# The bf16 conversion of the FFN's weights, issued in 64 pieces at every fourth step of attention instead of in 16 transfers

## The chip, the cores and the metric

The kernel runs on the 8 cores of one Trainium2 chip, one batch element on each core. A time is the device time of the slowest core in microseconds. The kernel before took 906.47 us (median of 3 runs).

## The reference

```python
# x: (8, 2048, 1024) f32; 16 heads of 64; FFN width 4096
def _L0_attn_ref(x, W_qkv, W_out):
    qkv = jnp.einsum('bsd,ndh->bnsh', x, W_qkv)
    q, k, v = jnp.split(qkv, 3, axis=-1)
    attn = jnp.einsum('bnqh,bnkh->bnqk', q, k) * scale
    attn = jax.nn.softmax(attn + causal_mask, axis=-1)
    out = jnp.einsum('bnqk,bnkh->bnqh', attn, v)
    out = out.reshape(B, -1, S)
    return jnp.einsum('bds,nhd->bsd', out, W_out)

def _L0_ffn_ref(x, w1, b1, w2, b2):
    h = jax.nn.relu(jnp.einsum('bsd,dw->bsw', x, w1) + b1)
    return jnp.einsum('bsw,wd->bsd', h, w2) + b2

x = x + _L0_attn_ref(_layernorm(x), L0_attn_W_qkv, L0_attn_W_out)
x = x + _L0_ffn_ref(_layernorm(x), L0_ffn_w1, L0_ffn_b1, L0_ffn_w2, L0_ffn_b2)
```

Attention's output is reshaped so that the last product sums W_out over heads and head positions; the kernel therefore needs no matmul for it, only a factor per element (WBp_sb).

## The kernel before

**Stages.** Each core works on a sequence of 2048 tokens by 1024 features. First come layer norm, transposes, the values of all heads and the queries and keys of the first pair of heads. Then comes attention, pair by pair: 8 pairs of heads, and in each 40 steps (`STEPS`), a step being a block of 512 queries (four of them) against a block of 128 keys as far as the causal mask lets it. Then comes the second layer norm and the FFN in 4 groups of 512 tokens, each with 32 blocks of the first product (line 514) and 8 of the second (line 536).

**A step of attention.** TensorE computes the scores of both heads two steps ahead (`score`, line 395, and the mask at line 407), ScalarE takes their exponential (line 626), and TensorE multiplies it with the values (`pv`, line 425). Between them TensorE computes the next pair's queries and keys (`qk`, line 371). The string `ORDER` writes out by hand how many halves of `pv` ("p") and pieces of `qk` ("f") stand in each step. VectorE evicts the next pair's queries (line 665) and applies the softmax's sums. TensorE counts finished scores in the semaphore `pe_s` (one per step, 320 in all), finished `qk` groups in `pe_f` (four per pair), and finished `pv` steps in `pe_pv`. Pair 7 has no next pair, so its steps hold no `qk`.

**The FFN's weights.** w1 and w2 lie in HBM as f32. The matmuls want bf16, and the conversion is done by transfers from HBM to HBM issued by GpSimd (POOL): w1 into `w1b` (line 281) and w2 into `w2b` (line 285), 8 transfers each of 1 MB of bf16. They are issued in `gpsimd`, in the loop that loads the queries' and keys' weights of pairs 1 to 7 into `wstage` (line 273). In its rounds 4, 5, 6 and 7, two transfers of w1 and two of w2 follow the load. Round 4 begins when the values are done, and rounds 5, 6 and 7 when the pairs 1, 2 and 3 have their queries and keys (`pe_f` 4, 8, 12). Everything that GpSimd issues goes through one queue (q0).

**Who waits for them.** The SyncE (SP) queue, in `sync`, waits at line 213 for all of w1, then at line 215 for `pe_f` 24 and 28, and loads the first two blocks of w1b (line 208). At line 217 it waits for all of w2 and loads w2b in four parts (line 222): two when `lnf_sb` is free, two when the last `pv` is done. GpSimd waits for both at its end (lines 295 and 296), behind the 16 additions of b2 to x (line 292), each of which waits for VectorE's second layer norm.

```python
STEPS = [(qb, j) for qb in range(4) for j in range(4 * qb + 4)]
NST = len(STEPS)
```

Of the kernel before, what the change touches and what calls it, by code (L numbers as in the profile page):

```python
# [11 lines left out]
AP = bass.AP  # L12

S = 2048
D = 1024
# [4 lines left out]
DC = 8  # L20
W1N = 4096
NWW = 32
# [7 lines left out]
NP = 5  # L30

WLAG, FLAG = 4, 7


ORDER = """
# [40 lines left out]
def build_program():  # L76
# [6 lines left out]
    w1_d = nc.dram_tensor("w1", [D, W1N], F32, kind="ExternalInput")  # L83
    b1_d = nc.dram_tensor("b1", [128, NWW], F32, kind="ExternalInput")
    w2_d = nc.dram_tensor("w2", [W1N, D], F32, kind="ExternalInput")
# [5 lines left out]
    w1b_d = nc.dram_tensor("w1b", [8, 128, DC * 512], BF16, kind="Internal")  # L91
    w2b_d = nc.dram_tensor("w2b", [128, NWW * D], BF16, kind="Internal")

    with ExitStack() as ctx:
# [3 lines left out]
        def sem(name):  # L98
            return ctx.enter_context(nc.semaphore(name))
# [60 lines left out]
        def slotap(s, dims):  # L160
            return AP(wstage, s * 1024, [[8 * 1024, 128]] + dims)
# [8 lines left out]
        w1_cast, w2_cast = sem("w1_cast"), sem("w2_cast")  # L170
# [6 lines left out]
        pe_s, pe_fh, pe_f = sem("pe_s"), sem("pe_fh"), sem("pe_f")  # L177
# [21 lines left out]
        def sync(e):  # L199
            for c in range(TC):  # L200
                e.dma_start(
                    x_sb[:, c, :], AP(x_d, c * 128 * D, [[D, 128], [1, D]])
                ).then_inc(x_in[c], 16)
            e.dma_start(b1c_sb[:, :], b1_d.ap()).then_inc(b1_in, 16)

            def w1_load(n):

                e.dma_start(
                    slotap(4 * (n % 2), [[1, DC * 512]]),
                    AP(w1b_d, (n % 8) * 128 * DC * 512, [[DC * 512, 128], [1, DC * 512]]),  # L210
                ).then_inc(w1b_in[n % 2], 16)

            e.wait_ge(w1_cast, 16 * 8)
            for n in range(2):
                e.wait_ge(pe_f, 24 + 4 * n)
                w1_load(n)
            e.wait_ge(w2_cast, 16 * 8)
            for i in range(4):
                if i == 2:
                    e.wait_ge(pe_pv, NSTEP)  # L220
                buf = lnf_sb if i < 2 else w2hi_sb
                e.dma_start(
                    AP(buf, (i % 2) * 8 * D, [[16 * D, 128], [1, 8 * D]]),
                    AP(w2b_d, i * 8 * D, [[NWW * D, 128], [1, 8 * D]]),
                ).then_inc(w2b_in[i], 16)
            for g in range(NG):
                for n in range(8 * g + 2, min(8 * g + 10, 8 * NG)):
                    e.wait_ge(pe_f1, 4 * (n - 2) + 4)
                    w1_load(n)
                for i in range(8 * g, 8 * g + 8):  # L230
                    e.wait_ge(dve_y, i + 1)
                    e.dma_start(
                        AP(y_d, (i // 2) * 128 * D + 512 * (i % 2), [[D, 128], [1, 512]]),
                        x_sb[:, i // 2, 512 * (i % 2):512 * (i % 2) + 512],
                    ).then_inc(y_out, 16)
            e.wait_ge(b1_in, 16)
            for c in range(TC):
                e.wait_ge(x_in[c], 16)
            for i in range(4):
                e.wait_ge(w2b_in[i], 16)  # L240
            for i in range(2):
                e.wait_ge(w1b_in[i], 16 * 16)
            e.wait_ge(y_out, 16 * 8 * NG)

        def gpsimd(e):
            e.dma_start(identb[:, :], identf_d.ap()).then_inc(cst_in, 16)
            e.dma_start(
                wqk0_sb[:, :], AP(wqk_d, 0, [[DC * 256, 128], [1, DC * 256]])
            ).then_inc(wqk0_in, 16)
            for h in range(2):  # L250
                if h == 1:
                    e.wait_ge(x_in[11], 16)
                    e.dma_start(maskd[:, :], maskd_d.ap()).then_inc(mask_in, 16)
                e.dma_start(
                    slotap(4 * h, [[1, DC * 512]]),
                    AP(wv_d, h * 128 * DC * 512, [[DC * 512, 128], [1, DC * 512]]),
                ).then_inc(wv_in[h], 16)
            e.wait_ge(x_in[TC - 1], 16)
            for k in range(4):
                e.dma_start(  # L260
                    wout_sb[:, 2 * k:2 * k + 2, :],
                    AP(wout_d, k * 256 * D, [[D, 128], [128 * D, 2], [1, D]]),
                ).then_inc(wout_in[k], 16)
            e.wait_ge(dve_ln, TC)
            e.memset(
                AP(v_all, 64, [[TC * NPAIR * 192, 128], [192, TC * NPAIR], [1, 64]]), 1.0
            ).then_inc(pool_ones)
            for n in range(1, NPAIR):
                if n <= 4:
                    e.wait_ge(pe_v, TC if n <= 2 else 2 * TC)  # L270
                else:
                    e.wait_ge(pe_f, 4 * (n - 4))
                e.dma_start(
                    slotap(2 * ((n - 1) % 4), [[1, DC * 256]]),
                    AP(wqk_d, n * 128 * DC * 256, [[DC * 256, 128], [1, DC * 256]]),
                ).then_inc(wqk_in[(n - 1) % 4], 16)
                if n == 4:
                    e.dma_start(b2_sb[:, :], AP(b2_d, 0, [[0, 128], [1, D]])).then_inc(b2_in, 16)
                if n >= 4:
                    for k in range(2 * n - 8, 2 * n - 6):  # L280
                        e.dma_start(
                            AP(w1b_d, k * 128 * DC * 512, [[DC * 512, 128], [512, DC], [1, 512]]),
                            AP(w1_d, 512 * k, [[W1N, 128], [128 * W1N, DC], [1, 512]]),
                        ).then_inc(w1_cast, 16)
                        e.dma_start(
                            AP(w2b_d, 4 * k * D, [[NWW * D, 128], [D, 4], [1, D]]),
                            AP(w2_d, 4 * k * 128 * D, [[D, 128], [128 * D, 4], [1, D]]),
                        ).then_inc(w2_cast, 16)
            e.wait_ge(b2_in, 16)
            for c in range(TC):  # L290
                e.wait_ge(dve_ln, TC + 4 * (c // 4) + 4)
                e.tensor_add(x_sb[:, c, :], x_sb[:, c, :], b2_sb[:, :]).then_inc(pool_b2)  # L292
            e.wait_ge(cst_in, 16)
            e.wait_ge(mask_in, 16)
            e.wait_ge(w1_cast, 16 * 8)
            e.wait_ge(w2_cast, 16 * 8)
            for i in range(4):
                e.wait_ge(wout_in[i], 16)
            e.wait_ge(wqk0_in, 16)
            for i in range(2):  # L300
                e.wait_ge(wv_in[i], 16)
            for i in range(4):
                e.wait_ge(wqk_in[i], 32 if i < 3 else 16)
# [467 lines left out]
        with nc.Block() as block:  # L771
            block.sync(sync)
            block.gpsimd(gpsimd)
            block.tensor(tensor)
            block.vector(vector)
            block.scalar(scalar)
# [37 lines left out]
```

## Time and profile before

| | us |
|---|---|
| median of 3 runs | 906.47 (903.72 to 908.82) |
| the profiled execution's own time | 910.64 |
| its span (slowest core, core 7) | 909.1 |
| spans of the eight cores | 894.7 to 909.1 |

The profile is of one execution. Its page shows the slowest core; a view can be had of each of the others. A span runs from the first instruction to the last, and the time is a little longer than the longest span. Times in the rows are counted from the start of a core's span. Queue 0 carries what GpSimd issues, queue 1 what SP issues, and queues 8 and 14 carry instructions. A wait for "issue" is idle time in which the engine waited for nothing that the profile shows. The granted clock is a share of full speed.

### The profile page before, as it was taken

How to read it: one execution, taken by the hardware profiler on the slowest of the kernel's cores; microseconds unless marked ns; L12 is line 12 of the kernel's file. 1: busy time of each engine (PE TensorE's matmuls, PEld its weight loads, DVE VectorE, ACT ScalarE, POOL GpSimd, SP SyncE). 2: the span in 40 equal slices, each digit the busy share in tenths (PEclk: the TensorE clock that was granted, in tenths of full speed). 3: DMA queues.
4: the chain of work that ended last, by engine and by line, in shares of the span. 5: the costliest groups of instructions: out<-in, count | busy, mean ns of one | idle time of the engine just before them, and what ended most of it. 6: DMA issues, size and time to landing. Idle time of an engine off the chain costs nothing.

```text
span 909.1 us, 14407 instructions; the slowest of 8 cores (894.7 to 909.1 us)
## 1 busy us (share of the span) xinstructions
PE 850.2 (94%) x5968; PEld 381.4 (42%) x5968; DVE 412.8 (45%) x672; ACT 357.3 (39%) x478; POOL 67.4 (7%) x54
## 2 busy tenths in 40 slices
PE   0899999989999999988399999999999999999998
PEld 0444444433444444432144444444444444444443
DVE  3560065865576776867655310653006520044210
ACT  1464389987899999999211000010000100000000
POOL 0103011010100000000034000040000400000000
PEclk9999999997999999999689999999999999999999
DMA  8962099999998001042423310233102340034001
GB/s 196 289 99 47 5 134 99 115 107 112 109 107 102 1 3 48 2 133 101 185 93 140 139 45 37 104 140 139 46 35 105 139 151 35 35 110 178 13 35 46
DMA packets 27808, 85.44 MB, mean 94 GB/s; under 512 B 2144, under 2 KB 10464, under 8 KB 22880
## 3 DMA queue, kind: packets, MB, share of 16 engines
q0 software_dynamic: 15504, 25.79, 23.7%
q1 hardware_dynamic: 12240, 58.74, 18.3%
q8 instruction: 47, 0.77, 0.3%
q14 instruction: 17, 0.14, 0.0%
HBM read 101.40 MB, written 25.17 MB: 139 GB/s over the span
## 4 chain that ended last, share of the span: by engine, by line
PE 91%; ACT 2%; DMA 2%; DVE 2%; issue 2%; DVEq 1%; SPq 0%; ACTq 0%
PE arena L514 25%; PE arena L536 24%; PE arena L425 14%; PE arena L371 11%; PE arena L395 7%; PE arena L327 6%; DMA x_sb<-x 2%; PE arena L348 2%; PE arenab L308 1%; ACT p_sb L626 1%; PE arena L407 1%; ACT lnf_sb L558 1%; DVE lntm_sb L659 0%; DVE bst_sb L649 0%; PE arena L468 0%
## 5 line engine op out<-in xcount | busy, mean ns | idle before, releaser
L626 ACT ACTIVATE p_sb<-arena 128x1024 bf16<-128x1024 f32 (+1 forms) x320 | 268.8, 905 | 23.3 <-PE arena L395 14.5
L514 PE MATMUL arena<-lnf_sb,wstage 128*128 128x512 bf16 x1024 | 225.3, 381 | 1.3 <-ACT lnf_sb L558 1.3
L425 PE MATMUL arena<-p_sb,v_all 64*128 64x512 bf16 (+3 forms) x1280 | 207.4, 356 | 7.0 <-issue 3.3
L514 PEld LDWEIGHTS arena<-lnf_sb,wstage 128*128 128x128 bf16 x1024 | 100.1, 98 | 120.6 <-issue 3.8
L371 PE MATMUL arena<-lnf_sb,wstage 64*128 64x512 bf16 x896 | 147.1, 385 | 1.4 <-issue 1.4
L753 DVE TENSOR_SCALAR h_sb<-arena,b1c_sb 128x512 bf16<-128x512 f32 x128 | 95.5, 746 | 106.1 <-PE arena L514 105.2
L395 PE MATMUL arena<-qpair,kpair 64*128 64x512 bf16 (+3 forms) x640 | 114.0, 354 | 5.3 <-ACT p_sb L626 5.2
L536 PE MATMUL arena<-lnf_sb,h_sb 128*128 128x512 bf16 x512 | 115.7, 379 | 0.0
L536 PE MATMUL arena<-w2hi_sb,h_sb 128*128 128x512 bf16 x512 | 115.7, 379 | 0.0
L767 DVE TENSOR_TENSOR x_sb<-arena,x_sb 128x512 f32<-128x512 f32 x32 | 22.1, 692 | 198.6 <-PE arena L536 198.6
L425 PEld LDWEIGHTS arena<-p_sb,v_all 64*128 64x128 bf16 x1280 | 53.3, 95 | 94.8 <-PE arena L425 69.7
L547 ACT ACTIVATE rsd_sb<-bag_sb,cst_sb 128x2 f32<-128x2 f32 (+1 forms) x12 | 3.5, 294 | 219.8 <-DVE bag_sb L652 219.5
L699 DVE TENSOR_TENSOR t_sb<-osc_sb,rec_sb 64x256 bf16<-64x256 f32 x128 | 76.4, 597 | 3.9
L536 PEld LDWEIGHTS arena<-w2hi_sb,h_sb 128*128 128x128 bf16 x512 | 50.1, 98 | 60.4
L536 PEld LDWEIGHTS arena<-lnf_sb,h_sb 128*128 128x128 bf16 x512 | 50.1, 98 | 60.4
L292 POOL TENSOR_TENSOR x_sb<-x_sb,b_sb 128x1024 f32<-128x1024 f32 x16 | 37.1, 2347 | 440.4 <-DVE lntm_sb L659 440.4
L371 PEld LDWEIGHTS arena<-lnf_sb,wstage 64*128 64x128 bf16 x896 | 43.7, 96 | 39.7 <-issue 6.1
L558 ACT ACTIVATE lnf_sb<-arenab 128x1024 bf16<-128x1024 bf16 x32 | 31.6, 1023 | 72.2 <-PE arenab L308 72.2
L308 PE MATMUL arenab<-identb_sb,lntm_sb 128*128 128x128 bf16 x256 | 21.7, 241 | 39.5 <-DVE lntm_sb L659 39.5
L327 PE MATMUL arena<-wstage,lnf_sb 128*128 128x512 bf16 x256 | 57.5, 382 | 0.0
L395 PEld LDWEIGHTS arena<-qpair,kpair 64*128 64x128 bf16 x640 | 32.1, 95 | 45.6 <-ACT p_sb L626 23.9
L671 DVE COPY osc_sb<-arena 128x512 f32<-128x512 f32 x32 | 22.0, 687 | 50.8 <-PE arena L425 50.5
(44 smaller groups left out, 420.9 us busy)
## 6 DMA issues: line engine op xcount, KB each, us to landing
wstage<-w1b SPq DMA_DIRECT2D x32, 1024.0 KB, 4.8
x_sb<-x SPq DMA_DIRECT2D x16, 512.0 KB, 21.0
w1b<-w POOLq DMA_DIRECT2D x8, 1024.0 KB, 42.0
w2b<-w POOLq DMA_DIRECT2D x8, 1024.0 KB, 48.8
y<-x_sb SPq DMA_DIRECT2D x32, 256.0 KB, 2.0
lnf_sb<-w2b SPq DMA_DIRECT2D x2, 2048.0 KB, 15.2
w2hi_sb<-w2b SPq DMA_DIRECT2D x2, 2048.0 KB, 12.0
wstage<-wqk POOLq DMA_DIRECT2D x7, 512.0 KB, 7.9
```

What stands on the lines that cost most here:

```text
L292: e.tensor_add(x_sb[:, c, :], x_sb[:, c, :], b2_sb[:, :]).then_inc(pool_b2)
L308: mm = e.transpose(AP(arenab, bank * 1024 + dc * 128, [[2 * AR, 128], [1, 128]]), lntm_sb[:, buf, dc * 128:(dc + 1) * 128], identb[:, :])
L327: mm = e.matmul(bankap(2 + u % 4), lnf_sb[:, dc, c * 128:(c + 1) * 128], AP(wstage, 4 * h * 1024 + dc * 512, [[8 * 1024, 128], [1, 512]]), ...
L371: mm = e.matmul(bankap(6 + isk), AP(wstage, r * 8192 + ((pair - 1) % 4) * 2048 + dc * 256 + isk * 128, [[8 * 1024, 64], [1, 128]]), lnf_sb ...
L395: mm = e.matmul(AP(arena, (bank + h) * 512 + off, [[AR, 128], [1, w]]), kpair[h * 64:(h + 1) * 64, pr, j * 128:(j + 1) * 128], qpair[h * 6 ...
L425: mm = e.matmul(AP(arena, (4 + h) * 512 + off, [[AR, 128], [1, w]]), v_all[r:r + 64, j, pair, 64 * h:64 * h + 128], AP(p_sb, r * NP * 1024 ...
L514: mm = e.matmul(bankap(ww % 4, TF), AP(wstage, 4 * ((n // 4) % 2) * 1024 + dc * 512 + (ww % 4) * 128, [[8 * 1024, 128], [1, 128]]), lnf2_s ...
L536: mm = e.matmul(bankap(6 + dh), h1_sb[:, ww, 128 * c2:128 * c2 + 128], w2ap(ww, 512 * dh), start=(ww == 0), stop=(ww == NWW - 1), skip_gro ...
L558: at(e.activation(dst, AP(arenab, bank * 1024, [[2 * AR, 128], [128, 8], [1, 128]]), AF.Identity), pe_tp, idx + 1).then_inc(act_lnf)
L626: at(e.activation(AP(p_sb, (n % NP) * 1024, [[NP * 1024, 128], [512, 2], [1, w]]), AP(arena, 2 * (n % 2) * 512 + off, [[AR, 128], [512, 2] ...
L699: e.tensor_mul(AP(t_sb, par * 64 * TC * 128 + h * 64 + 16 * qb, [[TC * 128, 64], [128, TC], [1, 16]]), AP(osc_sb, h * 64 * 2048 + (ep % 2) ...
L753: at(e.tensor_scalar(h1_sb[:, ww, :], bankap(ww % 4, TF), b1c_sb[:, ww:ww + 1], 0.0, op0=ALU.add, op1=ALU.max), pe_f1, NWW * g + ww + 1).t ...
```

## The change

The 16 transfers are cut into 64: w1 in pieces of 128 rows by two of the eight blocks, w2 in pieces of 128 rows. The rows and their lengths stay as they are, and so do the total bytes. Piece i waits for `pe_s` to reach 4 i + 1, that is for the score of step 4 i, on GpSimd. All 32 pieces of w1 come first, then the 32 of w2. Pieces 0 to 15 stand behind the load of round 4, 16 to 31 behind that of round 5, and so on. The waits for all of w1 or w2 count to 32 transfers instead of 8.

```diff
--- before.py
+++ after.py
@@ -31,6 +31,8 @@
 
 WLAG, FLAG = 4, 7
 
+NCAST, CAST = 16, 4
+
 
 ORDER = """
     pffff pf pfp ff
@@ -210,11 +212,11 @@
                     AP(w1b_d, (n % 8) * 128 * DC * 512, [[DC * 512, 128], [1, DC * 512]]),
                 ).then_inc(w1b_in[n % 2], 16)
 
-            e.wait_ge(w1_cast, 16 * 8)
+            e.wait_ge(w1_cast, 16 * 32)
             for n in range(2):
                 e.wait_ge(pe_f, 24 + 4 * n)
                 w1_load(n)
-            e.wait_ge(w2_cast, 16 * 8)
+            e.wait_ge(w2_cast, 16 * 32)
             for i in range(4):
                 if i == 2:
                     e.wait_ge(pe_pv, NSTEP)
@@ -276,15 +278,21 @@
                 ).then_inc(wqk_in[(n - 1) % 4], 16)
                 if n == 4:
                     e.dma_start(b2_sb[:, :], AP(b2_d, 0, [[0, 128], [1, D]])).then_inc(b2_in, 16)
-                if n >= 4:
-                    for k in range(2 * n - 8, 2 * n - 6):
+
+                for i in range(NCAST * max(n - 4, 0), NCAST * max(n - 3, 0)):
+                    e.wait_ge(pe_s, CAST * i + 1)
+                    if i < 32:
+                        k, q = divmod(i, 4)
                         e.dma_start(
-                            AP(w1b_d, k * 128 * DC * 512, [[DC * 512, 128], [512, DC], [1, 512]]),
-                            AP(w1_d, 512 * k, [[W1N, 128], [128 * W1N, DC], [1, 512]]),
+                            AP(w1b_d, k * 128 * DC * 512 + 1024 * q,
+                               [[DC * 512, 128], [512, 2], [1, 512]]),
+                            AP(w1_d, 512 * k + 256 * q * W1N,
+                               [[W1N, 128], [128 * W1N, 2], [1, 512]]),
                         ).then_inc(w1_cast, 16)
+                    else:
                         e.dma_start(
-                            AP(w2b_d, 4 * k * D, [[NWW * D, 128], [D, 4], [1, D]]),
-                            AP(w2_d, 4 * k * 128 * D, [[D, 128], [128 * D, 4], [1, D]]),
+                            AP(w2b_d, (i - 32) * D, [[NWW * D, 128], [1, D]]),
+                            AP(w2_d, (i - 32) * 128 * D, [[D, 128], [1, D]]),
                         ).then_inc(w2_cast, 16)
             e.wait_ge(b2_in, 16)
             for c in range(TC):
@@ -292,8 +300,8 @@
                 e.tensor_add(x_sb[:, c, :], x_sb[:, c, :], b2_sb[:, :]).then_inc(pool_b2)
             e.wait_ge(cst_in, 16)
             e.wait_ge(mask_in, 16)
-            e.wait_ge(w1_cast, 16 * 8)
-            e.wait_ge(w2_cast, 16 * 8)
+            e.wait_ge(w1_cast, 16 * 32)
+            e.wait_ge(w2_cast, 16 * 32)
             for i in range(4):
                 e.wait_ge(wout_in[i], 16)
             e.wait_ge(wqk0_in, 16)
```

## Rows read from the trace of the kernel before

**Rows 1.** The page: busy time, and of the 40 slices the clock and the DMA share.

```profile
PE 850.2 (94%) x5968; PEld 381.4 (42%) x5968; DVE 412.8 (45%) x672; ACT 357.3 (39%) x478; POOL 67.4 (7%) x54
...
PEclk9999999997999999999689999999999999999999
...
DMA  8962099999998001042423310233102340034001
```

**Rows 2.** Span and mean granted TensorE clock of three of the cores.

```profile
core 2: 894.7 us, clock 0.989
...
core 6: 904.8 us, clock 0.979
...
core 7: 909.1 us, clock 0.975
```

**Rows 3.** Line 665, the evictions of the queries, on cores 2, 6 and 7.

```profile
L665 DVE CAST qpair<-arena x28: 683/691/692, 119.2 to 383.4; 128x512 bf16<-128x512 f32 x28
...
L665 DVE CAST qpair<-arena x28: 683/691/692, 121.9 to 393.7; 128x512 bf16<-128x512 f32 x28
...
L665 DVE CAST qpair<-arena x28: 682/691/693, 120.6 to 397.7; 128x512 bf16<-128x512 f32 x28
```

**Rows 4.** Stages of core 7: us, busy of PE, PEld, DVE, ACT, POOL, PEclk, DMA share, GB/s.

```profile
109.50:298.00 188.50, 181.34 (x1913) 77.51 (x1913) 118.93 (x205) 165.36 (x213) 16.21 (x22) 0.94 0.96 107
298.00:398.00 100.00, 99.42 (x1102) 42.69 (x1100) 69.97 (x121) 94.97 (x122) 0.00 (x0) 1.00 0.03 12
```

**Rows 5.** Chain of waits, core 7: start us, us, what.

```profile
201.87 3.27 issue
...
244.82 1.44 issue
...
321.93 0.91 PE arena L371 x8
...
360.94 0.91 PE arena L371 x8
...
515.61 55.25 PE arena L536 x256
```

**Rows 6.** Waits of the score matmuls on cores 5, 6 and 2: us, times, longest.

```profile
PE arena L395 <- issue: 5.5, 3, 3.3
...
PE arena L395 <- issue: 1.0, 1, 1.0
...
PE arena L395 <- issue: 0.4, 1, 0.4
```

**Rows 7.** DMA queues of core 7 in 187.5 to 202.4, 202.5 to 203, 290 to 398 us.

```profile
q0 software_dynamic: 1157, 1.53, 100.7%
...
q8 instruction: 1, 0.02, 13.7%
...
q8 instruction: 9, 0.15, 0.5%
```

**Rows 8.** DMA queues and issues of core 7 from 109.5 to 291 us.

```profile
q0 software_dynamic: 13276, 19.67, 98.2%
...
w1b<-w POOLq DMA_DIRECT2D x8, 1024.0 KB, 42.0
```

**Rows 9.** Line 281 (issue on POOL), and line 273's time from issue to landing.

```profile
L281 POOL DMA_DIRECT2D w1b<-w x8: 888/964/1042, 113.0 to 240.9; - x8
...
DMA to landing us min/median/max: 5.1/7.9/26.6
```

**Rows 10.** Core 7 after the first hole, columns as in rows 4.

```profile
205.10:211.90 6.80, 6.70 (x42) 2.55 (x42) 1.26 (x2) 2.79 (x4) 0.00 (x0) 0.56 1.02 125
```

**Rows 11.** Core 6, columns as in rows 4.

```profile
109.50:298.00 188.50, 184.51 (x1967) 78.69 (x1966) 121.69 (x210) 169.94 (x219) 16.20 (x22) 0.96 0.94 107
```

**Rows 12.** SP: its wait for TensorE from 350 us, and its first w2 loads.

```profile
SPq L215 <- PE arena L371: 106.4, 2, 67.8
...
L222 SPq DMA_DIRECT2D lnf_sb<-w2b x2: 368/395/422, 398.1 to 398.6; - x2
```

## The prediction, made before the changed kernel was built

> **What bounds the kernel now.** The page comes first. TensorE is busy 94% of the span, so time is lost only where TensorE stands still or runs at a lower clock; in slices 6 to 13 the 16 DMA engines are full [rows 1]. The core comparison comes second, because the metric is the slowest core: the cores do the same work and end between 894.7 and 909.1 us, and core 7 is the last [rows 2]. The third view asks where they part. The first and the last eviction of the next pair's queries (line 665, 28 of them) stand at 119.2 and 383.4 us on core 2, at 121.9 and 393.7 on core 6, at 120.6 and 397.7 on core 7 [rows 3]. Between them lie 264.2, 271.8 and 277.1 us. After the last one come 511.3, 511.1 and 511.4 us: the rest of the kernel is the same on all three. So core 7 loses 12.9 us and core 6 loses 7.6 us against core 2 inside attention, and nowhere else.
>
> The stage table says when. From 109.5 to 298 us, with the DMA share at 0.96, core 7 has TensorE busy 181.34 of 188.5 us at a mean granted clock of 0.94; from 298 to 398 us, with the share at 0.03, 99.42 of 100 at 1.00 [rows 4]. The first stretch is that of the 16 weight transfers. The chain shows two holes there in which TensorE waits for nothing that the profile shows, 3.27 us at 201.87 and 1.44 us at 244.82 [rows 5]. The waits of score matmuls for "issue" come to 5.5 us on core 5, 1.0 on core 6 and 0.4 on core 2, which is the fastest [rows 6]. What ends such a hole can be seen in the DMA queues: queue 8 brings instructions in packets of 16 KB. None came in the 14.9 us from 187.5 to 202.4, where the queue of the transfers filled the engines, and the next came between 202.5 and 203, when TensorE had already stood since 201.87. In the quiet stretch 9 of them come in 108 us, one in 12 us [rows 7]. I read the hole as code that came 3 to 5 us late behind the weight transfers, which lie on the same 16 engines. They are deep: issued in bursts of four, and those of w1 take 42.0 us to land [rows 8]; a 512 KB load of query and key weights takes up to 26.6 us, where the quickest of the seven took 5.1 [rows 9].
>
> After the hole the granted clock falls: 0.56 from 205.1 to 211.9 us, mostly at the lower level of 1.2 GHz [rows 10]. A second loss is apart from it. Core 6 has one hole of 1.0 us, too short to explain its 7.6, but its granted clock averages 0.96 from 109.5 to 298 us [rows 11], against 1.00 in core 7's quiet stretch.
>
> **The change, part by part.** Edit 1: 16 transfers become 64 of a quarter of the size, with the same rows (2 KB in and 1 KB out for w1, 4 KB in and 2 KB out for w2), so the same 12,288 packets. Their time: queue 0 fills 98.2% of the 181.5 us from 109.5 to 291, 178 us, with 13,276 packets, 13.4 ns of the 16 engines each [rows 8]; 12,288 of these are 165 us, or 2.6 us for each of 64 pieces. I take no extra for the cut, since rows and engines are the same; the bounds are 2.6 us and the 5.1 us to landing of the quickest 512 KB load [rows 9]; below 2.6 us nothing speaks, as the packets stay. Even 5.1 us is latency that overlaps with the next piece.
>
> Edit 2: the wait. A piece goes out every fourth step. A pair has 40 steps and takes 39.0 us in the calm stretch (the chain's run of eight line-371 matmuls comes back at 321.93 and 360.94 us [rows 5]), so a piece is due every 3.9 us. The load falls from 0.98 to about 2.6/3.9 = 0.67 and what stands in the queue from up to four transfers (42 us) to one piece (2.6 us). The transfers end later: the last piece is due at step 252 of 320, 12 steps into the pair that now begins just before 360.94, so at 371 us by the old clock and near 358 with core 7's 12.9 us taken off, instead of 291. Its cover is SP's order: the w1 wait ends with the piece of step 124, near 233 us at 0.98 us a step, and SP stands for up to 67.8 us behind TensorE's line 371 anyway; the first w2 load goes out at 398.1 us (385 with the 12.9 off), still 27 us after the last piece [rows 12], and TensorE first reads w2 at 515.61 [rows 5]. If that cover were gone, a late w2 would still have some 100 us before it reaches the path. I cost it at nothing.
>
> Edit 3: what queues behind the waits on POOL. The three loads of query and key weights for pairs 5, 6 and 7 now stand behind pieces 15, 31 and 47, that is steps 60, 124 and 188, about 170, 233 and 295 us. They are read in pairs 4, 5 and 6, from about 268, 307 and 346 us: 50 to 100 us of slack against a landing of 5.1 to 26.6 us [rows 9]. The additions of b2 come after the last piece, and wait for VectorE's second normalization as before. Issuing a transfer costs POOL 0.89 to 1.04 us [rows 9], and at most that for a quarter of one: 64 issues are at most 67 us instead of 16, at least 16, and I take 40. POOL computes nothing then, so nobody waits for it. TensorE gets no instruction more, since it counts pe_s already.
>
> **The sum, on core 7 and then on the core that is last after it.** The profiled execution took 910.64 us, 1.55 over its span of 909.1 and 4.2 over the median of the runs. Holes 3.27 + 1.44 = 4.7 us, and 6.8 us at 0.56 lose 3.0: 7.7 us, which brings core 7 to 901.4. Core 5's holes are larger than core 7's (5.5 us in three), so I let it fall below core 6 too, which is then last: 904.8 [rows 2] less its hole of 1.0 is 903.8. Of its 7.6 us, 6.6 are left for the lower clock. No row shows that clock at a load of 0.67. The bounds are nothing recovered (as in the full stretch) and all (as in the quiet one), and the load lies between; I take somewhat over half, 4 us: core 6 at 899.8, and 901.3 with the 1.55 outside. The median may lie slightly under a run in which the holes were many, so I say 901.0, 9.6 under the profiled execution and 5.5 (0.6%) under the median. A difference of 0.5%, 4.5 us, is about what a measurement of this kernel can tell.
>
> A rule speaks against the larger term. The Trainium skill (Runtime: NRT & Kernel Launch, Instruction fetch mechanics) says that code comes in 16 KiB blocks on a DMA queue of its own and that crossing a block is mostly hidden. The 16 KB packets agree; the holes of 3.27 and 1.44 us do not. By the rule the 7.7 us would not be recovered.
>
> **The rivals.**
> Everything is recovered. No hole, and the clock at 1.00: core 6 at 121.9 + 264.2 + 511.1 = 897.2, time 898.7. For it: no stretch of low load shows a lower clock in attention. Against it: 0.67 is not low.
>
> The clock stays. The clock falls with TensorE's and the chip's work, and the holes alone go: core 6 at 903.8, time 905.4, 0.1% under the median. For it: the same bytes and the same matmuls. Against it: in the quiet stretch TensorE is busy 99.42 of 100 us at 1.00 [rows 4], and in the FFN the clock's digits are all 9 [rows 1]. The Trainium skill (TensorE: Matmul & The Clock Gate, under the HAM trace caveats) tells of a current limiter that takes a whole die to 13/16 because of its matmuls. By it transfers would not matter to the clock; the quiet stretch contradicts that.
>
> Nothing comes of it. The pieces bunch up (a piece takes as long as its spacing, or wqk loads and pieces meet), the engines are full again, the holes stay: 906.5. For it: a 512 KB load takes 5.1 us at best [rows 9], longer than 3.9.
>
> Slower: what delays the code is not the backlog but any row in front of it. Then holes and low clock go with the time in which pieces are in flight, not with their depth. That time grows from 178 us (113.0 [rows 9] to 291) to 245 (113 to 358), by 1.38; core 7's 12.9 us become 17.8, and the median 911.4. It decides from this point: code that comes 3 to 5 us late stops TensorE, and one piece is 2.6 us, two are 5.2. Against it: core 2 had the same 16 transfers for the whole stretch and 0.4 us of holes [rows 6], so lateness is at the edge already and a third of the load should pull it back. The Trainium skill (DMA: Bandwidth & Descriptors, Queues, rings and completion order) says that an engine takes turns between the queues that have work, a packet of some 9 to 17 descriptors at a time. By that rule depth would not matter, and this is the case that it speaks for; the 14.9 us without code agree with it badly.
>
> **How the numbers follow.** Forecast (holes go, part of the clock comes back) 0.46. All comes back 0.12. Clock stays 0.20. Nothing comes of it 0.14. Slower 0.08. The first two are faster: 0.58. The next two are within 0.5%: 0.34. The range takes in the whole recovery with 2 us for a run with fewer delays at the start, 896.5, and reaches up to the case of nothing, 906.5; above it lie the slower case and half of the case of nothing.
>
> **What would show it.** Right: the DMA share in attention near 0.7 until about 360 us on all cores and quiet after; 64 issues on POOL with landings of 4 to 8 us; no wait of a matmul for "issue" above 1 us between 110 and 360; the distance from the first to the last line-665 eviction within 3 us of 264 on every core of die 0; a spread of the cores of about 6 us instead of 14. Wrong: a hole of over 2 us with a 16 KB packet at its end; a granted clock below 0.97 between 300 and 358 us, where it was 1.00 (the slower case); a landing of 10 us or more (pieces bunch up); TensorE waiting at line 371 for wqk weights, or at line 536 for w2.

## The result, and the profile after

The changed kernel takes 897.46 us (median of 8 runs) against 907.08 us of the kernel before (median of 8): ratio 0.9905, 95% interval 0.9876 to 0.9934. Medians here are over all runs, a few of which were disturbed and took longer; ratios and counts of cores leave those out and rest on the others, the compared runs. The profiled execution took 898.6 us, its span is 897.1 us, and its eight cores lie between 892.6 and 897.1 us, where those of before lay between 894.7 and 909.1.

The page of the changed kernel (its slowest core, core 2): busy time, clock and DMA share by slices, and the issues with KB each and median us to landing.

```profile
PE 838.2 (93%) x5916; PEld 378.1 (42%) x5968; DVE 412.5 (46%) x672; ACT 355.5 (40%) x478; POOL 92.6 (10%) x102
...
PEclk9999999999999999999599999999999999999999
DMA  9963096785855746070533201333003330034001
...
w1b<-w POOLq DMA_DIRECT2D x32, 256.0 KB, 6.6
w2b<-w POOLq DMA_DIRECT2D x32, 256.0 KB, 4.6
```

Against [rows 1] the DMA digits of slices 7 to 16 are 4 to 8, where slices 6 to 12 were 9: less load over a longer time. A piece of w1 lands in 6.6 us where a whole transfer of w1 took 42.0 [rows 8].

Line 673 is line 665 of before. Its rows on cores 2, 6 and 7 (the first and the last start are what counts):

```profile
L673 DVE CAST qpair<-arena x28: 683/692/692, 120.6 to 384.0; 128x512 bf16<-128x512 f32 x28
...
L673 DVE CAST qpair<-arena x28: 683/691/693, 119.4 to 382.7; 128x512 bf16<-128x512 f32 x28
...
L673 DVE CAST qpair<-arena x28: 683/692/693, 117.1 to 380.6; 128x512 bf16<-128x512 f32 x28
```

The distance is 263.4, 263.3 and 263.5 us, and 263.3 to 263.5 on all eight cores. In [rows 3] it was 264.2, 271.8 and 277.1. Most of the gain lies there: what two cores of before lost in attention is gone, and even core 2's 264.2 was 0.8 too long.

Stages of core 7 after, columns as in [rows 4]: the transfers of pieces run through both stretches.

```profile
109.50:298.00 188.50, 187.06 (x2068) 80.38 (x2064) 131.96 (x228) 178.26 (x232) 32.31 (x53) 1.00 0.66 85
298.00:355.00 57.00, 56.55 (x656) 24.72 (x656) 38.68 (x68) 53.61 (x72) 7.73 (x15) 1.00 0.54 89
```

The share is 0.66 for 0.96, the clock 1.00 for 0.94, and TensorE is busy 187.06 us of 188.5. The chain of core 7 from 110 to 398 us has these steps at "issue" in the place of those in [rows 5] (start us, us, what):

```profile
198.33 0.40 issue
384.77 0.69 issue
```

Neither is what is left of a hole of before. The first stands where TensorE has started 3,063 instructions (the hole of 3.27 us stood at 3,003), and core 2 of before has it at the same place:

```profile
201.19 0.40 issue
```

The one at 384.77 stands in every core's chain, before too. In the stream of TensorE's instructions itself, no gap over 0.25 us is left between 118 and 382 us on any of the eight cores.

### The profile page after: what moved, and what is told of

Its sections match the earlier page's. It is cut to its first block, busy times and chain, and to the rows that moved or that the text cites. A ratio compares the mean times of both kernels' runs of the same rounds, so it can differ in the third digit from the quotient of the medians.

```text
span 897.1 us, 14467 instructions; the slowest of 8 cores (892.6 to 897.1 us)
## 1 busy us (share of the span) xinstructions
PE 838.2 (93%) x5916; PEld 378.1 (42%) x5968; DVE 412.5 (46%) x672; ACT 355.5 (40%) x478; POOL 92.6 (10%) x102
## 4 chain that ended last, share of the span: by engine, by line
PE 89%; DMA 3%; ACT 2%; DVE 2%; issue 2%; DVEq 1%; SPq 0%; ACTq 0%
PE arena L544 25%; PE arena L522 24%; PE arena L433 14%; PE arena L379 11%; PE arena L403 6%; PE arena L335 6%; DMA x_sb<-x 2%; PE arena L356 2%; PE arenab L316 1%; ACT p_sb L634 1%; DMA wstage<-w1b 1%; PE arena L415 1%; ACT lnf_sb L566 1%; DVE lntm_sb L667 0%; DVE t_sb L707 0%
## 5 line engine op out<-in xcount | busy, mean ns | idle before, releaser
L433 PE MATMUL arena<-p_sb,v_all 64*128 64x512 bf16 (+3 forms) x1280 | 202.2, 348 | 4.0 <-DVE osc_sb L679 0.6
L379 PE MATMUL arena<-lnf_sb,wstage 64*128 64x512 bf16 x896 | 143.5, 376 | 0.0
L403 PE MATMUL arena<-qpair,kpair 64*128 64x512 bf16 (+3 forms) x640 | 111.4, 346 | 5.3 <-ACT p_sb L634 5.2
## 6 DMA issues: line engine op xcount, KB each, us to landing
x_sb<-x SPq DMA_DIRECT2D x16, 512.0 KB, 20.8
wstage<-wqk POOLq DMA_DIRECT2D x7, 512.0 KB, 9.6
```

What stands on the lines that cost most here:

```text
L379: mm = e.matmul(bankap(6 + isk), AP(wstage, r * 8192 + ((pair - 1) % 4) * 2048 + dc * 256 + isk * 128, [[8 * 1024, 64], [1, 128]]), lnf_sb ...
L403: mm = e.matmul(AP(arena, (bank + h) * 512 + off, [[AR, 128], [1, w]]), kpair[h * 64:(h + 1) * 64, pr, j * 128:(j + 1) * 128], qpair[h * 6 ...
L433: mm = e.matmul(AP(arena, (4 + h) * 512 + off, [[AR, 128], [1, w]]), v_all[r:r + 64, j, pair, 64 * h:64 * h + 128], AP(p_sb, r * NP * 1024 ...
```

## What the holes are, read closer

The prediction read late code out of the time between two code packets. That was a weak reading, since this time varies anyway with how many instructions a step of `ORDER` holds. How far TensorE has come in its code when a packet begins says more. The 11th packet of 16 KB on queue 8 starts at 202.65 us on core 7 before and at 186.55 us after. These are the stretches up to it (before, then after; the counts behind PE and PEld are the matmuls and weight loads started):

```profile
0.00:202.65 202.65, 174.45 (x1446) 80.48 (x1446) 95.83 (x167) 128.68 (x184) 26.48 (x33) 0.98 0.77 121
```

```profile
0.00:186.55 186.55, 162.32 (x1334) 75.14 (x1334) 88.10 (x153) 118.51 (x170) 30.16 (x41) 1.00 0.66 117
```

The same packet comes when TensorE has started 2,892 matmuls and loads before, and 2,668 after, so before it is 224 instructions later. At some 22 a microsecond (2,202 in the 100 us of the quiet stretch in [rows 4]) that is 10 us. For all packets one number can be made, the position of the packet: all records of TensorE started when packet k begins less 256 k. k is counted from 0, so this packet is 10, and the records hold a few other instructions beside matmuls and loads: before, at this packet, they are 3,003, and the position is 443. In the quiet stretch of before, from 300 to 380 us, it is 194 on average. The table has it for 130 to 290 us, over the eight cores of each profile (110 to 115 packets each). The packet of core 7's other hole stands at 413.

```
                            mean  90th pct.  largest  400 and more
before                       317     413       443        16
after                        223     283       356         0
e1  pieces, bursts           312     357       418         1
e6  pieces, bursts, in turn  306     353       427         3
e3  pieces, every 3          275     320       391         0
e4  pieces, two in flight    230     274       356         0
e2  whole, every 16          245     331       415         1
e5  whole, bursts, w1 first  311     379       443         4
e10 the kernel of e5 again   312     388       442        10
e7  w2 doubled               315     391       443         8
e9  whole, every 10          311     378       443         4
e12 whole, two in flight     316     381       443         6
e8  three transfers          217     310       392         0
e11 the change again         223     278       372         0
```

Each row is one profile. e5 and e10 are one kernel and have 4 and 10 in the last column, so small differences there say nothing.

The place of the stops ties them to these packets. In the fourteen profiles TensorE stands still for more than 0.25 us 61 times between 118 and 382 us: 16 times before, 2 to 10 times in e1, e5, e6, e7, e9, e10 and e12, once each in e2 and e3, and never in the change, e4, e8 and e11. Every one of the 61 begins at the same place in the code, 443 records past 256 k (434 on the cores whose trace lacks some matmuls), and ends 0.6 to 1.6 us after packet k has ended. So TensorE comes to the end of the code that it has, and goes on when packet k is in.

That end is 249 instructions past the calm position, 11 us, but the packet has to begin earlier than that. No packet that began below 371 had a stop behind it, and none that began above 408 was without one. So TensorE bears code that is late by some 200 instructions, about 9 us, and not by 3 to 5 as I had it. Before, the mean packet was 5.6 us late ((317 - 194) / 22) and did no harm; the tail did.

## The experiments

Theories: **A**, the backlog in queue 0 delays the code; **B**, the size of one transfer does; **C**, full engines do, whatever stands in the queue. Ratios are against the kernel before on the same chip. The hole given for each run is the longest stop of TensorE in its profile.

### e1: the pieces without the pace

```diff
-                    e.wait_ge(pe_s, CAST * i + 1)
```

> The 64 pieces without the pace: the wait on pe_s is gone, so each of the four rounds issues its 16 pieces at once, gated only by pe_v and pe_f as the whole transfers were. Theory A (what delays the code is the backlog in the queue of the transfers, some 40 us deep): holes of 1 to 3 us in TensorE come back on most cores, the spread of the cores is over 8 us again, time 903 to 908. Theory B (the code waits for the rest of one transfer, whose rows an engine finishes before it turns to another queue; a piece has a quarter of them): no holes, time 897 to 900, although the DMA share is near 1.0. Theory C (the engines being full is what costs, however deep the queue): as A, 903 to 908.

Measured: 899.59 us, ratio 0.9951 (0.9925 to 0.9978). A piece took 33.2 us (w1) and 42.0 us (w2) to land, so the backlog is that of before, and the engines are full. Core 3, the longest of the profile, columns as in [rows 4]:

```profile
109.50:291.00 181.50, 177.76 (x1970) 76.65 (x1971) 122.52 (x211) 168.87 (x220) 41.21 (x70) 1.00 1.01 110
```

Its largest hole is 1.1 us. The cut without the pace brings half of the gain at a DMA share of 1.01 and a clock of 1.00. A and C fail as the only cause. B is near, but the holes are not all gone, and the mean position (312) is that of before: the cut shortens the tail, not the mean delay.

### e2: the pace without the pieces (and w1 first)

The 16 transfers as before, w1 first; `e.wait_ge(pe_s, 16 * i + 1)` ahead of transfer i.

> The 16 whole transfers as before, but one at every 16th step (w1 first, then w2): the pace without the pieces. Mean load 0.67 as with the change, one transfer of 10.6 us in flight at a time, and then 5 us of rest. A (backlog): code can be 5 to 10 us late behind one transfer, which is more than the 3 to 5 us that TensorE bears, so some holes: 899 to 903. B (rest of one transfer): holes as often as before while a transfer runs, two thirds as many: 901 to 905. C (full engines): a full stretch of 10 us is long enough for holes and for a lower clock, 901 to 905. If the pace alone is enough: 897 to 898 and no holes.

Measured: 898.81 us, ratio 0.9928 (0.9897 to 0.9958), largest hole 0.8 us. A transfer landed in 15.2 us (w1) or 12.9 us (w2). The DMA share is 0.58 to 0.73 on the cores. Whole transfers with the pace bring most of the gain too, so cut and pace don't add. But the order is changed with the pace here, and e5 shows below that the order has a part of its own. I had expected some holes; no core of six compared runs was over 897.5 us.

### e3: every third step

```diff
-NCAST, CAST = 16, 4
+NCAST, CAST = 16, 3
```

> As the change, but a piece every third step: 2.9 us between pieces of 2.6 us, DMA share near 0.9, backlog still about one piece. A: no holes, 897 to 898. C: most of the cost of full engines returns, 901 to 905, with holes and stretches of granted clock below 1.00. If the holes vanish with the load in proportion, about 900.

Measured: 898.33 us, ratio 0.9934 (0.9909 to 0.9958); DMA share 0.93 to 1.05 on the cores, w1 pieces landing in 12.5 us. The share is above what I had worked out (a piece takes nearly all of its 2.9 us), and still there is only one hole, of 1.0 us, on eight cores. C had 901 to 905 and fails as the cause of most of the loss. Full engines do delay the code: the mean position is 275 against 223 with the change, mostly below what TensorE bears.

### e4: pieces, two in flight, paced by their own landing

The edit in part (the semaphores `w1_cast` and `w2_cast` become two each, and their waits are split alike):

```diff
-                    e.wait_ge(pe_s, CAST * i + 1)
+                    if i < 2:
+                        e.wait_ge(pe_s, 1)
+                    elif i < 34:
+                        e.wait_ge(w1_cast[i % 2], 16 * (i // 2))
+                    else:
+                        e.wait_ge(w2_cast[i % 2], 16 * (i // 2 - 16))
```

> The 64 pieces paced by themselves: piece i goes out when piece i-2 has landed, with two semaphores for each weight, and no wait on pe_s. The engines are nearly full (share 0.85 to 1.0) for some 180 us as before, but never more than two pieces (5.2 us) are queued. A (depth): few or no holes, 897.5 to 900. C (load): 902 to 907, holes as before. B: as A.

Measured: 897.58 us, ratio 0.9911 (0.9882 to 0.9940), no hole, DMA share 0.74 to 0.83, landings 7.4 and 5.2 us. It equals the change without looking at attention's steps at all. The share stayed under what I wanted, so it says nothing of full engines.

### e5 and e10: the order alone

e1 and e2 also issue all of w1 ahead of all of w2. e5 has whole transfers in bursts in that order: `for i in range(4 * (n - 4), 4 * (n - 3))`, w1 for i under 8. e10 is the same kernel with more rounds.

> As the kernel before (16 whole transfers in four bursts, no pace), but the order of the first two runs of experiments: all 8 of w1, then all 8 of w2, where before they alternate. It takes apart what the pieces in bursts had mixed. If the cut did it: nothing changes here, 903 to 908, holes of 1 to 3 us. If the order did it (2 KB and 4 KB rows no longer mixed in the queue): 898 to 900 and next to no holes.

> The order alone once more (all of w1, then all of w2, whole, in bursts), with more rounds, since the first interval [0.9961, 1.0004] did not settle it. If the order has a part: 900 to 903, ratio 0.995 to 0.998 with 1 outside the interval. If it was chance: ratio 0.999 to 1.001.

Measured: 901.50 us, ratio 0.9983 (0.9961 to 1.0004), then 903.25 us, ratio 0.9973 (0.9946 to 1.0001). Both lean to faster, and neither interval leaves out 1. The time of the slowest core is a coarse measure, though, and the spans of all cores say more: the mean core of the compared runs takes 895.8 us in e5 and in e10, where the kernel before takes 898.0 and 897.6 on the same chips, and 15 and 17 of 72 core spans are over 897.5 us, where before it is 117 of 216 and 68 of 152. So the order has a part on either chip: it takes back about half of what the mean core loses (4 us), and less of the slowest core's time. With the transfers cut nothing of it shows (e1's mean core, w1 first, takes 895.2 us, e6's, in turn, 894.7).

### e6: the cut alone

The order and the bursts of before, with four pieces in place of each transfer.

> As the kernel before, in its order and bursts, but each transfer cut in four (64 pieces, four of w1, four of w2 and so on). If the cut did it (code waits for the rest of one transfer): 898 to 901, holes of at most about 1 us. If the order did it: 903 to 908.

Measured: 899.43 us, ratio 0.9944 (0.9915 to 0.9972), holes of 1.8 us on one core and at most 0.7 on the others. As e1, so the cut brings this much by itself, without the order.

### e7: w2 in 4 transfers of double size

> As the kernel before, but the 8 transfers of w2 are joined to 4 of twice the size (each round: w1, w1, w2 doubled). Same bytes, same rows, same bursts. If the size of a transfer sets how late code can come: more and longer holes than before, 908 to 915. If only the backlog or the full engines count: as before, 903 to 908.

Measured: 902.71 us, ratio 0.9999 (0.9967 to 1.0032). The expectation from B failed: no slower. Single holes are long, though. This is the longest row (us in total, times, longest), of core 2:

```profile
PE arena L395 <- issue: 4.4, 1, 4.4
```

A burst has now three transfers instead of four, w1, w1, w2. Since the order counts for something (e5), the changed mix of w1 and w2 may hide the size; this stays open.

### e8: three transfers only

It leaves out 13 of the 16 conversions and lets the FFN read the three converted blocks again.

> The floor: only 3 of the 16 transfers are issued (one of w1, two of w2, in the first burst), and the FFN reads these same blocks in place of the others; the conversion of the other 13 is left out. Everything else, loads of the FFN included, stays. If the change has won all that the transfers cost: 896.5 to 897.5, the time of the changed kernel within 0.1%. If the paced pieces still cost something: below 896.

Measured: 897.92 us, ratio 0.9929 (0.9902 to 0.9956), no hole, 263.2 to 263.4 us from the first to the last line-665 eviction. That is the changed kernel's time within 0.1% of 897.46. The pieces cost nothing that can be measured.

### e9: whole, in turn, one at every 10th step

The two lines added, with comments that are not in the kernel:

```diff
+                        e.wait_ge(pe_s, 20 * k + 1)   # before w1's transfer k
...
+                        e.wait_ge(pe_s, 20 * k + 11)  # before w2's transfer k
```

> The 16 whole transfers in the order of the kernel before (w1 and w2 in turn), one at every 10th step: 9.8 us between transfers of some 10.6 us, so the engines stay full as before, but one or two transfers are queued instead of up to four. Only the depth and the bursts of issues change. If a whole transfer in front of the code is what stops TensorE: 903 to 907, holes as before. If the deep queue or the burst of four issues is needed for it: 898 to 900. Together with the pieces in bursts (899.6) this fills the table of cut or whole, deep or shallow at full engines.

Measured: 903.03 us, ratio 0.9986 (0.9960 to 1.0012). The holes are there; on core 0 the chain has these (start us, us, what):

```profile
234.68 2.09 issue
...
273.14 1.13 issue
```

But this kernel was not what I meant it to be. Its issues (KB each, median us to landing) say so:

```profile
w1b<-w POOLq DMA_DIRECT2D x8, 1024.0 KB, 32.5
w2b<-w POOLq DMA_DIRECT2D x8, 1024.0 KB, 31.7
```

With 32 us to land, some three transfers were queued. What holds: without bursts of issues, but with a backlog and full engines, whole transfers in turn still cost what they cost before (the interval has 1 in it), where pieces at no less depth (e1) did not.

### e12: whole, in turn, two in flight

The lines ahead of w1's transfer k (those ahead of w2's are the same with `w2_cast`):

```diff
+                        if k > 0:
+                            e.wait_ge(w1_cast, 16 * k)
```

> What the pace of every 10th step was meant to be and was not (there a transfer took 32 us to land, so some three were queued): the 16 whole transfers in turn, each issued when the one before of its own kind has landed, so one of w1 and one of w2 are in flight and never more; engines full or nearly so. If full engines and whole transfers are enough for holes, whatever the backlog: 902 to 905, landings of 15 to 25 us. If it takes a deep backlog: 897.5 to 899.

Measured: 901.20 us, ratio 0.9944 (0.9907 to 0.9981); landings 21.4 and 21.0 us, DMA share 0.96 to 0.98. Core 0's chain has one hole (start us, us, what):

```profile
198.76 3.43 issue
```

It lies between the two outcomes that I had written down. Half the backlog brings about half of the gain, yet holes of 3.4 and, on core 2, 2.6 us still happen with two whole transfers in the queue and full engines.

### e11: the change once more

> The changed kernel itself beside the other two on one chip: 897 to 898, ratio 0.990 to 0.993, no core over 897.5 us in nearly all runs, and no hole over 0.5 us.

Measured, on the chip of e9 and e10: 896.92 us, ratio 0.9916 (0.9886 to 0.9947), largest hole 0.2 us, no core over 897.0 us in six compared runs.

### Together

Over all compared runs: how many core spans are over 897.5 us, the mean core span, and that of the kernel before on the same chips.

```
                                over 897.5    mean core    before, same chip
before (87 runs)                357 of 696    898.0
e9   whole, in turn, every 10    53 of  96    897.8        897.6
e7   w2 doubled                  27 of  80    896.8        898.0
e5, e10  order alone             32 of 144    895.8        898.0, 897.6
e12  whole, in turn, two          7 of  64    895.2        897.7
e1, e6   cut alone               13 of 136    895.2, 894.7 898.4, 898.0
e3   pieces, every 3              2 of  80    894.7        898.4
e2, e4, e8, e11, the change       0 of 264    893.7 to 894.3
```

The slowest of eight cores sets the time, and the holes strike the cores of a run nearly apart from each other. About half of before's core spans are over 897.5 us, but 86 of its 87 runs have at least one such core. So the median of the 87 is 7 us over the floor (904.6 against 897.5), although its mean core is only 4 us over (898.0 against the 893.8 of the change's cores and 894.1 of e8's).

## Why the prediction was right, and where not

**Where the time was.** Right. The loss was in attention during the transfers, as holes without a releaser that end when a code packet lands, plus the half clock behind them. Both went, and nothing of them came back between 298 and 355 us, where pieces now run.

**The sum.** I said 901.0 and the median is 897.46: what I called "Everything is recovered" (898.7, with a chance of 0.12) is what happened. The step that failed is the term for the lower clock. I let 2.6 of core 6's 6.6 us stay, "since no row shows that clock at a load of 0.67". None stayed. The other profiles don't tie that clock to the transfers: e1 has full engines (1.01) at 1.00, and e12, at 0.97, has 0.99 to 1.00. In the 87 compared runs of before that stood beside the experiments, no core has a mean clock under 0.983, where the profiled execution had 0.975 and 0.979 [rows 2]. The trace of before says it too. Cores 3 to 7 from 188.5 to 193 us, and then cores 6 and 7 from 38.5 to 42 us, columns as in [rows 4]:

```profile
188.50:193.00 4.50, 4.50 (x56) 1.94 (x54) 1.14 (x2) 4.18 (x5) 0.00 (x0) 1.00 1.09 108
188.50:193.00 4.50, 4.44 (x62) 2.19 (x60) 0.69 (x1) 3.73 (x6) 2.07 (x4) 0.81 0.99 104
188.50:193.00 4.50, 4.50 (x46) 1.79 (x44) 1.29 (x2) 4.21 (x5) 0.00 (x0) 0.81 1.07 95
188.50:193.00 4.50, 4.50 (x44) 1.84 (x44) 1.31 (x3) 4.21 (x5) 0.00 (x0) 0.81 1.07 106
188.50:193.00 4.50, 4.44 (x55) 1.90 (x52) 0.69 (x1) 3.68 (x7) 1.49 (x3) 0.81 1.02 106
...
38.50:42.00 3.50, 3.50 (x27) 2.11 (x26) 0.00 (x0) 2.63 (x4) 0.00 (x0) 0.81 1.18 198
38.50:42.00 3.50, 3.50 (x15) 1.50 (x14) 0.36 (x1) 2.46 (x5) 0.00 (x0) 0.82 1.14 209
```

A clock of 0.81, between the two levels, is granted to all four cores of die 1 at once, where core 3 and the rest of die 0 have 1.00 at the same full engines. On cores 6 and 7 the first such stretch comes at 38 us, some 70 us before the first weight transfer. No core of the other thirteen profiles has one. So the loss belonged to the one execution that was profiled, and what brought it on stays open; what hit all runs were the holes. I had taken it into the sum because the low clock and the transfers ended together. On core 7 the same clock took the 5.2 us of its 12.9 that my sum leaves over.

That 901.0 is as near as it is, is in part luck. 4.0 of the 9.6 us that I took off the profiled execution are a share of a clock loss that other runs don't have. In their place stand the holes on whichever core is last, which cost the median 7 us. What is left on core 6 is small. Of the 4.6 us down to its 892.6 us (899.8 less 2.6 less 892.6), 2.5 are an earlier first eviction (119.4 for 121.9), 1.2 a shorter rest (509.9 for 511.1), and 0.9 the 263.3 for 264.2.

**The cost of the pieces.** Right: 2.6 us each (a piece every 3.9 us gives a share of 0.67, and it is 0.66 on core 7), POOL 0.68 us for a w1 piece and 0.52 for a w2 piece, 38 us in all where I took 40. The last is issued at 357.3 us where I had 358. The floor (e8) confirms the nothing at which I put the change's own cost.

```profile
L293 POOL DMA_DIRECT2D w2b<-w x32: 515/515/544, 236.1 to 357.3; - x32
```

**The cause.** Half right. I put the lateness down to the backlog. That the holes are late code is now shown, by their place 443 records past 256 k. What makes it late is not the backlog alone. The whole loss takes a deep queue, full engines and whole transfers in turn: halving the backlog (e12, ratio 0.9944) or cutting the transfers (e6, 0.9944; e1, 0.9951) each takes about half of it off the time, and the order alone takes about half off the mean core (e5, e10). Cut with a shallow queue (e4, the change), or whole at a load of 0.58 to 0.73 with w1 first (e2), leaves no core over 897.5 us. The bound "code that comes 3 to 5 us late stops TensorE" was too small; it is about 9.

**The slower rival**, holes in proportion to the time in which pieces are in flight, is out: that time grew to about 245 us and the holes went. The Trainium skill's rule that carried it (DMA: Bandwidth & Descriptors, Queues, rings and completion order: an engine takes turns between queues by packets) fares better than I allowed. A packet was on average no later behind 42 us of pieces than behind whole transfers (312 and 317), and only 5 to 6 us late behind a backlog of 40: the code doesn't wait for the whole queue. The rule of the Trainium skill on code fetch (Runtime: NRT & Kernel Launch, Instruction fetch mechanics: mostly hidden) holds in the mean and fails in the tail, which is where the 7 us were.

**What is late next.** The slowest core of the profile, core 2, ends 513.1 us after its last query eviction, where others take 509.7 to 512.1. A late load of w1b in the FFN is in its waits (us in total, times, longest):

```profile
PE arena L522 <- DMA wstage<-w1b: 1.1, 1, 1.1
```

That is 1.1 of the 3.4 us between 513.1 and 509.7; cores 5 and 7 take 512.1 and 512.0 without such a wait, and what delays them is not shown.

**Open:** why the order of w1 and w2 has a part (e5, e10), how much of e2's gain is the pace and how much the order, why doubled transfers of w2 cost no more (e7), and what inside an engine makes a whole transfer's tail longer at the same mean. No run looked at a single DMA engine.

## What to carry to other kernels

When cores that do the same work end apart, compare them with each other first: the fastest core is the floor, and the difference tells what chance takes away. A background transfer that has time to spare (the last piece is issued some 27 us ahead of the first load of w2b here, and nothing waited) is better cut and paced, one or two small pieces in flight or one every few steps: deep queues of whole transfers made TensorE's code late enough here for stops of up to 4.4 us. When an engine stops without a releaser, count its instructions at the stop; stops that share one place in the code blocks point at the code and not at the data. And a loss that shows in one profiled execution should be held against the spans and clocks of the other runs before it goes into a sum.

## What the runs showed that I had not expected

TensorE bears code that is some 200 instructions late (about 9 us) without a stop, and every stop begins at one place, 443 records past 256 k. At full engines (a share of 1.01) 64 pieces in bursts still left the longest core's attention within 1.2 us of the floor (264.5 against 263.3 us). The order of whole transfers, w1 first instead of in turn, was worth 2 us of the mean core. And granted clocks of 0.81, on four cores of one die at once in the one profile, were absent from all the other profiles, at whatever load.
